# Transposing one query tile's attention probabilities by DMA instead of on TensorE, in an adaptive-norm transformer block

## What is computed

```python
x = L0_attn_hidden_states
sa, ca, ga, sb, cb, gb = ...  # from silu(c) @ wmod
h = layernorm(x) * (1 + ca) + sa
x = x + ga * attention(h, Wq, Wk, Wv, Wo)      # 32 heads of 64, 8 key heads, causal, rotary
h = layernorm(x) * (1 + cb) + sb
x = x + gb * ffn(h, ...)                        # top 2 of 8 experts, as low-rank parts on shared w1, w3, w2
```

```python
logits = einsum('bhqd,bhkd->bhqk', q, k) * scale
logits = where(causal, logits, finfo.min)
out = einsum('bhqk,bhkd->bhqd', softmax(logits), v)
return out.transpose(0, 2, 1, 3).reshape(b, s, H * HD) @ Wo.T
```

## Time and profile before

| | us |
|---|---|
| median of 3 runs | 491.07 |
| lowest and highest run | 490.6, 491.9 |
| profiled execution, its own time | 492.04 |
| its span, first to last instruction | 490.2 |
| mean granted TensorE clock | 0.979 of full |

### The profile page before, as it was taken

The page is one execution under the profiler, slowest core; times in us unless marked ns, Lnnn a source line. Parts: engine busy times, 40 slices in busy tenths (PEclk is TensorE's granted clock), DMA queues, the critical chain, the costliest instruction groups (busy, mean ns, idle before and its releaser), DMA issues.

```text
span 490.2 us, 12249 instructions
## 1 busy us (share of the span) xinstructions
PE 442.5 (90%) x4504; PEld 317.1 (65%) x4504; DVE 366.1 (75%) x1020; ACT 350.5 (72%) x636; POOL 331.6 (68%) x256
## 2 busy tenths in 40 slices
PE   3786989989999999999989998998898897999985
PEld 3363667777877878787868876787664453554453
DVE  3687868879888879888886997998747657633645
ACT  3425999979799889989986889899426556523331
POOL 4125799996779986769999679724326445583573
PEclk9985999999999999999998999999999998999999
DMA  8146241675343667333437414372110000000001
GB/s 295 69 117 212 81 130 45 172 192 166 98 112 64 173 115 175 102 94 102 130 88 195 98 55 109 82 181 40 27 23 0 2 0 0 2 1 0 23 22 45
DMA packets 57276, 44.60 MB, mean 91 GB/s; under 512 B 36608, under 2 KB 48896, under 8 KB 57216
## 3 DMA queue, kind: packets, MB, share of 16 engines
q1 hardware_dynamic: 55728, 41.70, 32.1%
q10 hardware_dynamic: 1488, 2.10, 1.2%
HBM read 23.87 MB, written 11.53 MB: 72 GB/s over the span
## 4 chain that ended last, share of the span: by engine, by line
POOL 33%; PE 30%; issue 14%; ACT 9%; DVE 8%; DMA 3%; SPq 1%; POOLq 0%; ACTq 0%; DVEq 0%
PE ps L480 7%; POOL av_l L1472 5%; PE ps L406 4%; POOL rot L1432 4%; POOL raw L1413 4%; POOL rot L1413 4%; PE ps L408 4%; PE ps L407 4%; POOL gsum L1533 3%; PE ps L462 3%; PE ps L464 3%; POOL rot L1424 3%; POOL on_l L1437 2%; ACT prob L834 2%; DMA oT<-on_l 2%
## 5 line engine op out<-in xcount | busy, mean ns | idle before, releaser
L1147 DVE CUSTOM_DVE_ANT_0 prob<-ps,causal 128x512 f32<-128x512 f32 (+3 forms) x256 | 117.8, 484 | 9.0 <-PE ps L464 7.2
L834 ACT ACTIVATE prob<-prob,least 128x512 f32<-128x512 f32 (+3 forms) x256 | 122.5, 555 | 0.6 <-DVE least L1147 0.6
L1155 DVE SCALAR_TENSOR_TENSOR pl<-ps,ph 128x512 f16<-128x512 f32 (+1 forms) x128 | 105.0, 821 | 22.2 <-ACT ph L841 19.0
L841 ACT ACTIVATE ph<-ps 128x512 f16<-128x512 f32 (+1 forms) x128 | 87.0, 702 | 27.0 <-PE ps L480 24.7
L480 PE MATMUL ps<-ident,prob 128*128 128x128 f32 x640 | 82.6, 276 | 1.8 <-ACT prob L834 0.9
L462 PE MATMUL ps<-kT_h,qT 128*128 128x512 f16 (+3 forms) x256 | 77.0, 303 | 6.5 <-DMA qT<-spill 3.4
L480 PEld LDWEIGHTS ps<-ident,prob 128*128 128x128 f32 x640 | 69.7, 142 | 3.2 <-DVE pl L1155 1.9
L464 PE MATMUL ps<-kT_l,qT 128*128 128x512 f16 (+3 forms) x256 | 70.7, 303 | 0.0
L500 PE MATMUL ps<-vh,ph 128*128 128x65 f16 x640 | 64.9, 194 | 0.5 <-DVE pl L1155 0.4
L502 PE MATMUL ps<-vl,ph 128*128 128x64 f16 x640 | 64.9, 193 | 0.0
L504 PE MATMUL ps<-vh,pl 128*128 128x65 f16 x640 | 64.8, 193 | 0.0
(11 more groups left out here) (180 smaller groups left out, 1031.9 us busy)
## 6 DMA issues: line engine op xcount, KB each, us to landing
spill<-rot SPq DMA_DIRECT2D x20, 512.0 KB, 3.9
qT<-spill SPq DMA_DIRECT2D x16, 512.0 KB, 3.8
wst<-chunks SPq DMA_DIRECT2D x30, 256.0 KB, 3.9
kT_h<-spill SPq DMA_DIRECT2D x8, 256.0 KB, 4.2
oT<-wmod ACTq DMA_DIRECT2D x3, 512.0 KB, 11.6
kT_l<-spill SPq DMA_DIRECT2D x4, 256.0 KB, 4.7
raw<-chunks SPq DMA_DIRECT2D x4, 256.0 KB, 4.6
out<-xs SPq DMA_DIRECT2D x4, 256.0 KB, 2.2
```

What stands on the lines that cost most here:

```text
L834: act.activation(prob[:, m % 2, c], prob[:, m % 2, c], ACT.Exp, bias=least[:, m % 2, qt:qt + 1], scale=-1.0).then_inc(exp_done, 1)
L841: act.activation(ph[:, m % 2, c], ps[:, PT_BANK:PT_BANK + 3, :].rearrange("p a b -> p (a b)")[:, c], ACT.Copy, scale=PROB_SCALE).then_inc( ...
L1147: ins = dve.tensor_tensor_reduce(prob[:, m % 2, at:at + w], ps[:, bank, off:off + w], causal[:, S - w:S], -1.0 / HD ** 0.5, 3.0e38, ALU.ad ...
L1155: dve.scalar_tensor_tensor(out=pl[:, m % 2, c], in0=ps[:, PT_BANK:PT_BANK + 3, :].rearrange("p a b -> p (a b)")[:, c], scalar=PROB_SCALE, ...
```

## The change

Tile 3's probabilities no longer go through TensorE. ScalarE rounds them from `prob` to a high half `rh` by rows (`rows_high`), VectorE makes `rl` (`rows_low`), and the SP queue transposes both by DMA into columns 0 to 511 of `ph` and `pl` (`transpose_rows`). `rh` and `rl` have one buffer each. TensorE transposes the other six blocks; the high and low halves of these are made in one part of 768 columns. The output sums go to bank 2, which tile 3's transposes had. The sums of a rotation come one period after its products. The last six feed-forward chunks are split two periods later, and the first batch's residuals are added in periods 38, 41, 44 and 45.

```diff
-PARTS = (slice(0, 512), slice(512, PROBS))
+ROWS, REST = slice(0, 512), slice(512, PROBS)
-SPLIT_AT = [...] + [30 + 2 * i for i in range(FFN_CHUNKS)]
+SPLIT_AT = [...] + [30 + 2 * i + 2 * (i > 3) for i in range(FFN_CHUNKS)]
-LATE_OUT = (58, 60, 62)
-def out_bank(n):
-    return 7 if n in LATE_OUT else 5
+RESIDUAL_AT = (38, 41, 44, 45)
+OUT_BANK = 2
+        rh, rl = (at_sb(f"r{k}", [P, 512], F16) for k in "hl")
+        rows_landed = [sem(f"rows_landed{i}") for i in range(2)]
...
+            def transpose_rows(m):
+                sp.wait_ge(rl_ready, m + 1)
+                wait(sp, pv_done, m - 1)
+                if m < 2:
+                    sp.wait_ge(xnT_mm, 2 * DK)
+                for to, t in ((ph, rh), (pl, rl)):
+                    sp.dma_start_transpose(to[:, m % 2, ROWS].rearrange("p (t c) -> p t c", t=T),
+                                           t[:, :]).then_inc(rows_landed[m % 2], 16)
...
                         fetch_item(it)
+                if 0 <= n + 2 < HEADS:
+                    transpose_rows(n + 2)
+                for it in range(DIRECT, len(ITEMS)):
                     if n == ITEM_AT[it] + 4:
                         spill_item(it)
...
             def transpose_probs(m):
-                wait(pe, pl_ready, 2 * m - 1)
+                wait(pe, pl_ready, m)
-                for i, qt in enumerate((3, 2, 0, 1)):
-                    if i == 1:
-                        wait(pe, pl_ready, 2 * m)
-                    pe.wait_ge(exp_done, 4 * m + i + 1)
+                for i, qt in enumerate((2, 0, 1)):
+                    pe.wait_ge(exp_done, 4 * m + i + 2)
...
             def values(m):
-                pe.wait_ge(pl_ready, 2 * m + 2)
+                pe.wait_ge(pl_ready, m + 1)
+                pe.wait_ge(rows_landed[m % 2], 32 * (m // 2 + 1))
-                if m > 10 and out_bank(m - 1) == PV_BANK:
-                    pe.wait_ge(op_added, (m - 9) // 2)
...
-                    if out_bank(n) == PV_BANK:
-                        pe.wait_ge(normed, n + 1)
-                    else:
-                        pe.wait_ge(op_added, (n - 10) // 2)
-                        if n == LATE_OUT[0]:
-                            pe.wait_ge(fs["h2h"], DK)
-                    output((n - 10) // 8, (n - 10) % 8 // 2, out_bank(n))
+                    if n == 10:
+                        pe.wait_ge(hh_ready, 2 * DK)
+                    wait(pe, op_added, (n - 10) // 2)
+                    output((n - 10) // 8, (n - 10) % 8 // 2, OUT_BANK)
...
+            def rows_high(m):
+                act.wait_ge(exp_done, 4 * m + 1)
+                wait(act, rows_landed[(m - 1) % 2], 32 * ((m + 1) // 2))
+                act.activation(rh[:, :], prob[:, m % 2, ROWS], ACT.Copy, scale=PROB_SCALE).then_inc(rh_ready, 1)
...
-                    probs_high(n + 1, 0)
-                    probs_high(n + 1, 1)
+                    probs_high(n + 1)
                 if 0 <= n + 2 < HEADS:
                     exps(n + 2, (3, 2, 0, 1))
+                    rows_high(n + 2)
...
-                if f == 0:
-                    wait(dve, pt_done, 2 * m - 2)
+                if f == 1:
+                    wait(dve, pt_done, m - 1)
...
+            def rows_low(m):
+                dve.wait_ge(rh_ready, m + 1)
+                dve.scalar_tensor_tensor(out=rl[:, :], in0=prob[:, m % 2, ROWS], scalar=PROB_SCALE,
+                                         in1=rh[:, :], op0=ALU.mult, op1=ALU.subtract).then_inc(rl_ready, 1)
...
-                if 0 <= n + 1 < HEADS:
-                    probs_low(n + 1, 0)
...
                 if 0 <= n + 1 < HEADS:
-                    probs_low(n + 1, 1)
+                    probs_low(n + 1)
+                if 0 <= n + 2 < HEADS:
+                    rows_low(n + 2)
...
+                for it in range(DIRECT, len(ITEMS)):
+                    if ITEM_AT[it] + 2 == n:
+                        rope_sums(it)
                 for it in range(DIRECT, len(ITEMS)):
                     if ITEM_AT[it] + 4 == n:
                         rotated_low(it)
...
                     if ITEM_AT[it] + 1 == n:
                         rope_products(it)
-                        rope_sums(it)
...
-                if n in (38, 40, 42, 44):
-                    residual_first((n - 38) // 2)
+                if n in RESIDUAL_AT:
+                    residual_first(RESIDUAL_AT.index(n))
```

More of the change, by code:

```diff
@@ L52 @@
 CHUNK_OF = {c: i for i, c in enumerate(CHUNKS)}
-SPLIT_AT = [None] * 5 + [-2, -1, 1, 3, 5, 7, 8, 9, 11, 13, 14, 18, 20, 24, 28] + [30 + 2 * i for i in range(FFN_CHUNKS)]
+SPLIT_AT = [None] * 5 + [-2, -1, 1, 3, 5, 7, 8, 9, 11, 13, 14, 18, 20, 24, 28] + [30 + 2 * i + 2 * (i > 3) for i in range(FFN_CHUNKS)]
 TILES, ITEMS = [], []
@@ L264, in block_kernel @@
             sem(k) for k in ("s_done", "maxed", "exp_done", "pt_done", "ph_ready", "pl_ready", "pv_done"))
+        rh_ready, rl_ready = sem("rh_ready"), sem("rl_ready")
+        rows_landed = [sem(f"rows_landed{i}") for i in range(2)]
         rsum_ready, normed, onh_ready, onl_ready = (sem(k) for k in ("rsum_ready", "normed", "onh_ready", "onl_ready"))
@@ L480, in transpose_probs @@
                         mm = pe.transpose(ps[:, PT_BANK + c // 512, c % 512:c % 512 + P], prob[:, m % 2, c:c + P], ident[:, :])
-                    if i in (0, 3):
-                        mm.then_inc(pt_done, 1)
+                mm.then_inc(pt_done, 1)
             def values(m):
@@ L626, in h_base @@
                 elif i == 1:
-                    pe.wait_ge(pl_ready, 2 * HEADS)
+                    pe.wait_ge(pl_ready, HEADS)
+                    pe.wait_ge(op_added, 27)
                 else:
@@ L835, in exps, with probs_high @@
                                    scale=-1.0).then_inc(exp_done, 1)
-            def probs_high(m, part):
-                act.wait_ge(pt_done, 2 * m + part + 1)
+            def probs_high(m):
+                act.wait_ge(pt_done, m + 1)
                 wait(act, pv_done, m - 1)
-                c = PARTS[part]
-                act.activation(ph[:, m % 2, c], ps[:, PT_BANK:PT_BANK + 3, :].rearrange("p a b -> p (a b)")[:, c],
+                act.activation(ph[:, m % 2, REST], ps[:, PT_BANK:PT_BANK + 3, :].rearrange("p a b -> p (a b)")[:, REST],
                                ACT.Copy, scale=PROB_SCALE).then_inc(ph_ready, 1)
+            def rows_high(m):
+                act.wait_ge(exp_done, 4 * m + 1)
+                wait(act, rows_landed[(m - 1) % 2], 32 * ((m + 1) // 2))
+                act.activation(rh[:, :], prob[:, m % 2, ROWS], ACT.Copy, scale=PROB_SCALE).then_inc(rh_ready, 1)
             def output_high(p):
@@ L1150, in row_max, with probs_low @@
                 ins.then_inc(maxed, 1)
[L1152 to L1156, removed]
-                                         scalar=PROB_SCALE, in1=ph[:, m % 2, c], op0=ALU.mult, op1=ALU.subtract)\
+            def probs_low(m):
+                dve.wait_ge(ph_ready, m + 1)
+                dve.scalar_tensor_tensor(out=pl[:, m % 2, REST],
+                                         in0=ps[:, PT_BANK:PT_BANK + 3, :].rearrange("p a b -> p (a b)")[:, REST],
+                                         scalar=PROB_SCALE, in1=ph[:, m % 2, REST], op0=ALU.mult, op1=ALU.subtract)\
                    .then_inc(pl_ready, 1)
+            def rows_low(m):
+                dve.wait_ge(rh_ready, m + 1)
+                dve.scalar_tensor_tensor(out=rl[:, :], in0=prob[:, m % 2, ROWS], scalar=PROB_SCALE,
+                                         in1=rh[:, :], op0=ALU.mult, op1=ALU.subtract).then_inc(rl_ready, 1)
             def norm(m):
@@ L1184, in _ @@
                 if n > 10 and n % 2 == 1:
-                    op_add((n - 11) // 8, (n - 11) % 8 // 2, out_bank(n - 1))
+                    op_add((n - 11) // 8, (n - 11) % 8 // 2, OUT_BANK)
                 if 0 <= n + 2 < HEADS:
                     row_max(n + 2, 1)
-                if 0 <= n + 1 < HEADS:
-                    probs_low(n + 1, 0)
                 if n >= 0:
```

## The result

The changed kernel takes 596.3 us in the median of 4 runs (592.9 to 598.95) against 491.25 us for the kernel before (4 runs): a ratio of 1.214, 95% interval 1.209 to 1.219. Slower was forecast, at 572 us, and the time lies inside the range of 515 to 604.

What follows compares the result with a forecast made beforehand. TensorE was taken to set the pace at 4.757 us a head. Loop 333.3, fetches 43.0 and keys 4.5 sum to 380.8 us for the attention stretch, 81.2 more than before: 572 us in all, range 515 to 604.

Steps and rivals of the forecast that it cites:

- TensorE's 0.44 us: Four of ten transposes a head leave TensorE: at most 27.7 us over 63 heads, not seen once the loop binds.
- The new loop: Single row buffers tie each head's copies to the previous head's landings: 5.29 us a head against 4.757, 333.3 us in all.
- the three hand-overs: Semaphore hand-overs between the engines and queue of the loop: 0.24 us together, bounds 0 and 0.48.
- rows_low at 0.69: VectorE's low-half copy in the loop, timed from the nearest SBUF subtraction of its shape, 686 ns: 0.69 us.
- the 17 fetches: Fetches ahead of the rows on the SP queue, waiting for spills and adding traffic: 43.0 us, plus 4.5 for three keys.
- the output transposes: 31 pairs on the SP queue, 2.5 us every second head, fitting in the gap behind the rows: nothing.
- The loop alone: Rival: fetches land in slack, so only the loop costs time, 33.7 us: 525 us; chance 0.21.
- The clock rival: TensorE's clock drops after stalls in the 17 fetch periods, 28.9 us more: 601 us; chance 0.14.
- Faster: Rival: transfers hidden and TensorE still the bound, so its 27.7 us are gained: 463 us; chance 0.03.
- no difference: Rival: transfer pairs of 3.2 us put the loop at today's pace; chance 0.02.
- The rule of X-Bar Transpose (TRN2): Transpose DMAs as fast as regular ones: 0.37 us per 128 KB, loop 2.3 us, never binding; the prediction went against it.
- The other edits: Output sums in the freed bank, rotations over two periods, later chunks and residuals: nothing, the bank at best 7.0 us.

Runs made afterwards that it cites:

- e8: Kernel before with only the edits that need no row transposes (later rotation sums, late chunks, residuals): 486.4 us, ratio 0.989.
- e4: Changed kernel with rows_low from head 4 on reading its full-precision input from PSUM bank 2 instead of SBUF: 593.2 us, ratio 1.196.
- e12: e9 with rows_low from head 4 on reading its full-precision input from PSUM bank 2: 482.7 us, ratio 0.982.
- e7: Changed kernel with four of the six TensorE transposes of each head done twice: 607.7 us, ratio 1.229.
- e11: Changed kernel with two pairs of row buffers for most heads, row transposes first on SP, copies earlier, a landing semaphore per half: 533.8 us, ratio 1.086.
- e9: Changed kernel without row transposes, both copies written straight into ph and pl, untransposed: 502.2 us, ratio 1.022.

## Why the prediction was right, and where it was off

**What bounds it, and TensorE's 0.44 us.** Right for the change: 640 transposes became 384, and nothing of their 27.7 us was seen as long as the transfers were there. For the kernel before it is half of the truth. The prediction read the chain in a calm window; over the whole stretch GpSimd holds nearly as much of it as TensorE (see e8), so not all of the 27.7 us were there to be had from TensorE alone.

**The new loop.** Right in mechanism and size: 5.29 us forecast, 5.18 measured in clean turns. The pair of transposes took 1.24 + 2.48 us against 1.24 + 2.50; the three hand-overs are 0.03, 0.03 and, from the landing to `rows_high`, 0.08 us, not the 0.24 together that I took. That is 63 x 0.11 = 7 us less than the 333.3 forecast: 326.3.

**rows_low at 0.69.** The single term that was furthest off: "the nearest SBUF subtraction of this shape takes 686". It does in the clean case (691 to 693 in the median), but 21 of 64 took 0.77 to 2.61 us, 17.1 us in all above 0.69. I had looked for the duration and not for what the instruction shares. The low half of before had one SBUF input, its other one being in PSUM; `rows_low` has two. So has the subtraction of the earlier trace rows, but both of its instances there ran with GpSimd idle. It has two more, behind the window of those rows. The line in the whole trace of the kernel before (ns min/median/max):

```profile
L1277 DVE TENSOR_TENSOR tm_l<-tm,tm_h x4: 680/688/1470, 368.3 to 419.7; 128x512 f16<-128x512 f32 x4
```

The one of 1470 ns began at 419.67, while GpSimd ran a subtraction, and ended 0.55 us behind it. The warning stood in the trace of before.

The timelines of VectorE and GpSimd side by side, around 74 us in the changed kernel:

```profile
72.02 2.61 DVE L1172 SCALAR_TENSOR_TENSOR rl<-prob,rh 128x512 f16<-128x512 f32 x1 [1.36 <-ACT rh L853]
```

```profile
71.73 2.35 POOL L1428 TENSOR_TENSOR rot<-raw,cos_sb 128x1024 f32<-128x1024 f32 x1
74.04 2.81 POOL L1428 TENSOR_TENSOR raw<-raw,sin_sb 128x1024 f32<-128x1024 f32 x1
```

GpSimd's rotation ends at 74.08, the copy at 74.63. In all 21 stretched copies the end lies 0.54 to 0.56 us behind the end of the GpSimd instruction that ran when the copy began. GpSimd's next instruction pays too, 2.81 us where the same form takes 2.35. The Trainium skill says this in SBUF — State Buffer, Who interferes with whom: a VectorE instruction with two SBUF inputs contends with a GpSimd instruction that reads SBUF, one with at most one SBUF input, outside the two-port modes, doesn't. The trace agrees with both halves, the second in e4 and e12, where 60 of 60 took about 0.69 us although 22 and 43 of them began while GpSimd ran.

**The SP queue.** 47.5 us forecast for the 17 fetches; their turns cost 43.5. That it comes so near is luck in part, for two errors cancel: a fetch alone cost 1.3 us and not 2.53, and a fetch with an output pair ahead of the rows 2.9, with a key item 4.5 (forecast 4.03). The term that failed is the one put at nothing, for the output transposes. They don't always fit in the gap behind the rows: of the 30.9 us ahead of the first issue, 25.4 lie in the ten turns with a fetch and an output pair, 3.5 in the seven with a fetch alone. The turns without a fetch cost 15.8 us more, where the prediction had nothing. Together it is 59.3 us, a quarter over the forecast.

**The sum, redone.** 326.3 + 17.1 + 59.3 = 402.7, for 402.99 measured and 380.8 forecast. The 22 us between forecast and measurement are 17 of `rows_low` and 12 of the queue, less the 7 of the loop.

**What the prediction didn't see.** The second loop, over two heads, through `values`. It didn't change the sum, since the loop of one head accounts for all of it. It does decide what removing that loop is worth: 37 us and not 71.

**The rivals.** The loop alone (525) fell: 59.3 us of waits and traffic came on top of it, for the fetches did not land in slack. The clock rival came nearest in time, 601, for the wrong reason. The granted clock did fall from 0.979 to 0.920 in the mean; after stalls it went to its lower level, 1.2 GHz, as in the earlier trace rows. Windows of 2 us in the changed kernel (columns as in the earlier trace rows):

```profile
326.00:328.00 2.00, 0.00 (x0) 0.00 (x0) 0.00 (x0) 0.00 (x0) 0.00 (x0) 0.94 0.98 200
328.00:330.00 2.00, 0.10 (x3) 0.13 (x4) 0.00 (x0) 0.10 (x1) 0.00 (x0) 0.50 0.81 111
```

But the sum above closes without it: the parts are the two copies, the queue and the landings, and `rows_high` started later than 0.08 us behind the landing by 2.4 us in all. And e7 raised the clock and got slower. Faster and no difference are excluded by a shortest turn of 5.17 us. The rule of X-Bar Transpose (TRN2) in the Trainium skill, Advanced Engine Details and Errata, which would have given the faster case, has transposes as fast as plain DMAs, by bandwidth. The trace doesn't agree for 128 KB: what counts here is issue and landing, 3.7 us a pair, where the prediction's estimate from that rule was 0.37 us for each half. Large transfers, for which it may hold, no run here shows.

**The other edits.** Put at nothing, they are worth 4.9 us by e8 (491.25 to 486.35), from long steps that GpSimd's late rotations had made; what is left of them in the change wasn't tried. The freed bank by itself wasn't tried, since nothing frees it without the rows.

**What stays open.** How the 3.8 us between e12 (482.7) and e8 (486.4) divide: less TensorE work, the freed bank, halves made in one piece, the difference behind the last maximum. And how much of e11's remaining 42 us over the kernel before is the stretched copies (21 us above 0.69 each, summed) and how much the queue; the SP queue and DMA hold 16% of its chain between the first and the last maximum.

## What to carry to other kernels

Before moving work from a busy engine to DMA, write down every buffer that the transfer reads and who waits for it to be free: copy, issue, landing and copy again is a loop, and it must be shorter than the period, whatever the prefetch distance of the result. One queue in order makes every wait in it a wait of all that stands behind, so a transfer on the loop must not share it with one that waits for others. And when an operand moves from PSUM to SBUF, ask how many SBUF inputs the instruction then has, and what GpSimd is doing at that time.

## What the runs showed of the hardware

- A VectorE instruction of 0.69 us with two SBUF inputs stretched to as much as 2.92 us (e9) beside GpSimd's 2.35 us multiplications, ending some 0.55 us after them; never with one of the inputs in PSUM (120 instructions in e4 and e12, 65 of which began while GpSimd ran). In e9, with VectorE busier, it added up to 34 us; taking it away gave 19.5 us.
- The semaphore hand-overs from ScalarE to VectorE and from VectorE to the SP queue took 0.03 us each, less than the 0.08 and 0.16 us read in the earlier trace rows; from a landing to ScalarE it was 0.08 us.
- The median from issue to landing of a transpose did not change with their number: 2.5 us, for 32 pairs as for 96. Beside other traffic it did: 24 of the 64 low halves landed 2.8 to 4.35 us after their issue.
